# Six-layer local-attention transformer in one kernel: two output projections one step later, and three of them ahead of the turn

## The chip, the cores and the metric

The kernel runs on one core of one Trainium2 chip. The metric is the device time in microseconds (us). The core's engines are named as the profile names them: PE (TensorE; PEld is its weight load), DVE (VectorE), ACT (ScalarE), POOL (GpSimd) and SP (SyncE, which here only issues DMAs). Each engine runs its own instructions in the order written and waits on semaphores for the others.

## The reference

`x` is [2, 1024, 128]. Two blocks follow each other, `x = x + s * silu(g)`; in each, `s` is an attention over a layer norm of `x`, and `g` is in the first block a mixture of experts and in the second a transformer of six layers. The change touches only that transformer. One of its layers, with the tokens' right half of channels shifted by one token first:

```
qkv = shift(x) @ Wqkv                       # 128 -> 3 * 1024, 16 heads of 64
q, k = l2norm(q) * qs, l2norm(k) * ks, both rotated by a rotary table with scale
sim = 8 * q @ k^T, banded: query i sees keys i-32 .. i
x = softmax(sim) @ v @ Wo + x
a, gate = split(layernorm(shift(x)) @ W1 + b1)
x = (a * gelu(gate)) @ W2 + b2 + x
```

All of it is float32.

## The kernel before

The program is a sequence of stages. `stage_transformer` is the next to last; it takes the last 1976 us of a span of 3707 us.

**Passes and steps.** A pass `n` (0 to 23) does 8 of the 16 heads of one batch element in one layer. `j = n % 4` says which: half of the heads `h = j // 2`, batch element `b = j % 2`. A pass has 11 steps `s`, one for each tile of 96 queries. Token tiles of 128 (8 of them, `t`) are what is projected and turned. Passes with `j` 3 or 0, except pass 0, are *feeding*: they also carry the feed-forward of the batch element whose attention has just been finished, spread over their steps 0 to 5 (`feed_step`). There are 11 of these; the other 13 are called plain here. Passes 1 to 20 run in a hardware loop of five turns of four passes.

**What a step holds on PE**, in this order (`run` of the tensor block):

- `scores(n, s)` (L1943): 8 small products of keys and queries into banks SC0 and SC1. It waits until both copies of the youngest token tile that it reads are made (`qk_ready`). For step 1 that is the tile turned in step 0, for step 5 the one turned in step 4, for step 8 the one turned in step 7; in the other steps the tile was turned earlier.
- `weigh(n, j, s - 1)`: the softmax's sum (L1976, "den"), then weights times values (L1985, "num") for the tile before. It waits for the exponentials of that tile.
- `turn` (L1996) in steps 0 to 5, 7, 8 and, for the next pass, 10: PE transposes one token tile of normalized queries into bank X1, then of keys into bank X0; ACT copies each out (L2161 queries, L2164 keys).
- `project` (L1957, queries and keys into banks PQ and PK) and `values` (L1964, into X0, copied out by ACT L2138) in steps 1, 2, 3, 5, 6 and, for the next pass, 8, 9, 10.
- `project_out` (L2006): the output projection of 192 queries (the last one 64), four products that add up in X1. DVE adds the result to `x` (`add_out`, L2283), which frees X1 (`x_added`). It runs in steps 3, 5, 7, 9, and the last two parts in steps 0 and 1 of the next pass.
- in feeding passes the step's piece of the feed-forward: step 0 and 4 `up` (L2035, needs X0 and X1 both), step 1 and 5 `down` (L2045, X0), step 2 `mean_of` (L2014, X0), step 3 `variance` (L2020, X0).

**Banks.** X0 and X1 are shared by many users. `take(x)` makes PE wait until the last user of the bank has been read by its reader; `free[x]` holds which semaphore and count that is. A wait of PE stops all that is behind it.

**ACT in a step:** `invert` (L2143, L2145: logarithm and exponential of the softmax's sum, for the tile before), `roots` (L2150, L2152, L2155: the l2 norms of the tile projected in the step before), `copy_turned` (L2161, L2164), `squares` (L2129) and `copy_v` (L2138), `exps` (L2120: exponentials of this step's scores), and in feeding passes its part of the feed-forward (L2173, L2175 after the variance; the gelus L2181 with a table load).

**DVE in a step:** `mask` (L2266: scores plus band), `outputs` (L2274: num times the inverse sum), `rotate` (L2258, L2259, L2260, twice each: rotary products and sums of squares), `add_out` (L2283), and in feeding passes its part of the feed-forward (L2307, L2309 normalize; L2316 gate; L2323 feed).

**POOL** adds the rotary products and scales them into `nq` (L2421, L2428), which `turn` reads after waiting for `nq_ready`.

Of the kernel before, what the change touches and what calls it, by code (L numbers as in the profile page):

```python
# [11 lines left out]
P = 128  # L12
# [1741 lines left out]
WIN = 32  # L1754
# [10 lines left out]
OUTS = 6  # L1765
# [4 lines left out]
PROJ_NEXT_AT = {8: 0, 9: 1, 10: 2}  # L1770
TURN_AT = {0: 1, 1: 2, 3: 3, 4: 4, 5: 5, 7: 6, 8: 7}
TURN_NEXT_AT = {10: 0}
OUT_AT = {3: 0, 5: 1, 7: 2, 9: 3}


def out_width(e):
# [23 lines left out]
def stage_transformer(nc, d, ident, yT):  # L1800

    with Stage(nc, "tr") as st:
# [20 lines left out]
        qT = st.sb("qT", [P, NPAIR, S])  # L1823
        kT = st.sb("kT", [P, NPAIR, XW])
# [12 lines left out]
        ps = st.ps("ps", [P, 8, CH])  # L1837
# [6 lines left out]
        summed, nq_ready, turned, qk_ready = S_("summed"), S_("nq_ready"), S_("turned"), S_("qk_ready")  # L1844
# [13 lines left out]
        SC0, SC1, NUM, DEN, PQ, PK, X0, X1 = range(8)  # L1858
# [67 lines left out]
        def _(pe):  # L1926
            free = [None, None]
# [40 lines left out]
            def weigh(n, j, s):  # L1968

                a = NQT * n + s  # L1970
                width = tile_width(s)
                slot = (j + s) % 2
                pe.wait_ge(exp_done, a + 1)
                at_least(pe, o_ready, a)
                for e in range(2):
                    mm = pe.matmul(ps[e * DH:(e + 1) * DH, DEN, 0:NPAIR * QT], ones[:], pr[:, slot, e, :], start=True,  # L1976
                                   stop=True, tile_position=(0, e * DH), skip_group_check=True)
                mm.then_inc(den_done, 1)
                t = (QT * s + width - 1) // P
                for u in range(max(t - 1, 0), t + 1):  # L1980
                    pe.wait_ge(v_tiled[u % 2], 16 * tiled_count(n, u))
                for p in range(NPAIR):
                    for e in range(2):
                        head = 2 * p + e
                        mm = pe.matmul(ps[e * DH:(e + 1) * DH, NUM, p * QT:p * QT + width],  # L1985
                                       v[:, s, head * DH:(head + 1) * DH], pr[:, slot, e, p * QT:p * QT + width],
                                       start=True, stop=True, tile_position=(0, e * DH), skip_group_check=True)
                mm.then_inc(num_done, 1)

            def turn(n, t):  # L1990
                g = NTT * n + t
                for i, x in ((0, 1), (1, 0)):
                    take(x)
                    pe.wait_ge(nq_ready, 2 * g + 1 + i)
                    for p in range(NPAIR):
                        mm = pe.transpose(ps[:, X0 + x, p * P:(p + 1) * P], nq[:, t % 2, i, p * P:(p + 1) * P], ident[:])  # L1996
                    mm.then_inc(turned, 1)
                    free[x] = (qk_ready, 2 * g + 1 + i)

            def project_out(n, h, e):  # L2000
                width = out_width(e)
                slot = 2 * (e % 2) * QT
                take(1)
                pe.wait_ge(o_ready, NQT * n + min(2 * e + 2, NQT))
                for p in range(NPAIR):
                    mm = pe.matmul(ps[:, X1, 0:width], w[:, h, 3 * HC + p * P:3 * HC + (p + 1) * P],  # L2006
                                   o[:, p, slot:slot + width], start=(p == 0), stop=(p == NPAIR - 1))
                mm.then_inc(out_done, 1)
                free[1] = (x_added, OUTS * n + e + 1)
# [55 lines left out]
            def run(n, L, j, first=False, last=False):  # L2065
                h, b = j // 2, j % 2
                feeding = (j == 3 or j == 0) and not first
                if first:
                    for t in range(3):
                        project(0, 0, 0, t)  # L2070
                        values(0, 0, t)
                    turn(0, 0)
                free[0] = (qk_ready, 2) if first else (v_copied, NTT * n + 3)
                free[1] = (qk_ready, 2 * NTT * n + 1)
                for s in range(NQT):
                    scores(n, s)
                    if s:
                        weigh(n, j, s - 1)
                    elif not first:
                        weigh(n - 1, j - 1, NQT - 1)  # L2080
                    if s in TURN_AT:
                        turn(n, TURN_AT[s])
                    if s in TURN_NEXT_AT and not last:
                        turn(n + 1, TURN_NEXT_AT[s])
                    if s in PROJ_AT:
                        if feeding and s in (1, 5):
                            f = 2 * L if j == 3 else 2 * L - 1
                            pe.wait_ge(h_ready, 3 * (2 * f + s // 4) + 2)
                        project(n, L, j, PROJ_AT[s])
                        values(n, j, PROJ_AT[s])  # L2090
                    if s in PROJ_NEXT_AT and not last:
                        project(n + 1, L if j < 3 else L + 1, (j + 1) % 4, PROJ_NEXT_AT[s])
                        values(n + 1, (j + 1) % 4, PROJ_NEXT_AT[s])
                    if s in OUT_AT:
                        project_out(n, h, OUT_AT[s])
                    if s < 2 and not first:
                        project_out(n - 1, ((j - 1) % 4) // 2, OUTS - 2 + s)
                    if feeding:
                        feed_step(s, L if j == 3 else L - 1, 2 * L if j == 3 else 2 * L - 1,
                                  NTT * n + (3 if s == 0 else 6))  # L2100
                    if h == 1 and s == 8:
                        mean_of(2 * (2 * L + b), 0)
                    if h == 1 and s == 9:
                        variance(2 * (2 * L + b), 0)
# [4 lines left out]
            n = 4 * DEPTH  # L2109
# [7 lines left out]
        def _(act):  # L2117
# [37 lines left out]
                act.activation(rn[:, t % 2, :], rn[:, t % 2, :], ACT.Exp, scale=-0.5,  # L2155
                               bias=ln256[:, 0:1]).then_inc(rn_ready, 1)

            def copy_turned(n, t):
                g = NTT * n + t
                act.wait_ge(turned, 2 * g + 1)  # L2160
                act.copy(qT[:, :, t * P:(t + 1) * P], ps[:, X1, :].rearrange("p (a c) -> p a c", c=P)  # L2161
                         ).then_inc(qk_ready, 1)
                act.wait_ge(turned, 2 * g + 2)
                act.copy(kT[:, :, WIN + t * P:WIN + (t + 1) * P], ps[:, X0, :].rearrange("p (a c) -> p a c", c=P)  # L2164
                         ).then_inc(qk_ready, 1)

            def center_squares(k, c):
                act.wait_ge(centered, k + 1)
# [27 lines left out]
            def run(n, L, j, first=False, last=False):  # L2196
                h, b = j // 2, j % 2
                feeding = (j == 3 or j == 0) and not first
                if first:
                    for t in range(3):  # L2200
                        squares(0, t)
                        copy_v(0, t)
                        if t < 2:
                            roots(0, t)
                    copy_turned(0, 0)
                for s in range(NQT):
                    if s:
                        invert(n, s - 1)
                    elif not first:
                        invert(n - 1, NQT - 1)  # L2210
                    if s - 1 in PROJ_AT:
                        roots(n, PROJ_AT[s - 1])
                    if s - 1 in PROJ_NEXT_AT and not last:
                        roots(n + 1, PROJ_NEXT_AT[s - 1])
                    if s == 0:
                        roots(n, 2)
                    if s in TURN_AT:
                        copy_turned(n, TURN_AT[s])
                    if s in TURN_NEXT_AT and not last:
                        copy_turned(n + 1, TURN_NEXT_AT[s])  # L2220
                    if s in PROJ_AT:
                        squares(n, PROJ_AT[s])
                        copy_v(n, PROJ_AT[s])
                    if s in PROJ_NEXT_AT and not last:
                        squares(n + 1, PROJ_NEXT_AT[s])
                        copy_v(n + 1, PROJ_NEXT_AT[s])
                    exps(n, j, s)
                    if feeding:
                        feed_step(s, 2 * L if j == 3 else 2 * L - 1)
                    if h == 1 and s == 8:  # L2230
                        center_squares(2 * (2 * L + b), 0)
                    if h == 1 and s == 9:
                        deviations(2 * (2 * L + b), 0)
# [9 lines left out]
        def _(dve):  # L2243
# [112 lines left out]
            def run(n, L, j, first=False, last=False):  # L2356
# [5 lines left out]
                for s in range(NQT):  # L2362
# [7 lines left out]
                    if s in PROJ_NEXT_AT and not last:  # L2370
                        rotate(n + 1, PROJ_NEXT_AT[s])
                    if s in OUT_AT:
                        add_out(n, b, OUT_AT[s])
# [276 lines left out]
```

## Time and profile before

| | |
|---|---|
| median of 3 runs | 3710.39 us (3702.64 to 3718.77) |
| the profiled execution's own time | 3709.09 us |
| its span, first to last instruction | 3707.4 us |
| PE busy over the span | 2992.1 us (81%) |
| DVE, ACT, POOL busy | 2466.2 (67%), 2083.8 (56%), 1285.4 (35%) |
| mean granted TensorE clock | 0.906 |

Busy time is the time in which an engine's own instructions run; an engine that waits on a semaphore is not busy. Times of single instructions in the rows below are counted from the start of the span. PE's matmuls are pipelined: a group's listed duration reaches about 0.1 us into the next group, so the distance of two starts is what a group costs. In float32 each matmul shows as two records (x8 for four products).

### The profile page before, as it was taken

What the parts mean: (1) busy time and instruction counts of PE and PEld (TensorE: products, weight loads), DVE (VectorE), ACT (ScalarE), POOL (GpSimd) and SP (SyncE); (2) the same over time, 40 slices, a digit from 0 to 9 for tenths busy, and PEclk for the clock granted to TensorE, in tenths of its full rate; (3) what the DMA queues carried; (4) which work ended last, traced back from release to release, by engine and by line L of the source; (5) the groups of instructions that cost most, each with busy time, mean ns of one, the idle gap of its engine ahead of it and who ended that gap; (6) DMA issues with size and microseconds to landing.
All of it is one profiled execution on the core that took longest, in us unless ns stands there. A gap on an engine that the chain in (4) does not pass through costs nothing. (4 is left out here: it accounts for less than half of the span.)

```text
span 3707.4 us, 71470 instructions
## 1 busy us (share of the span) xinstructions
PE 2992.1 (81%) x22883; PEld 1620.1 (44%) x22883; DVE 2466.2 (67%) x4021; ACT 2083.8 (56%) x3805; POOL 1285.4 (35%) x1223
## 2 busy tenths in 40 slices
PE   2688887239738888845999999999999999999997
PEld 1332332113312223313665565566556556655653
DVE  6788888562347777765666666666666666666664
ACT  1477677112204666633666666666666666666664
POOL 0000000004323556624553354345435434544540
PEclk6588789569957999977999999999999999999998
DMA  5221121114231111232111111111111111111111
GB/s 197 84 85 55 62 73 60 56 45 108 67 38 30 35 34 34 37 68 99 38 54 31 49 54 31 42 45 51 34 49 49 35 42 45 49 31 53 38 35 42
DMA packets 195211, 200.31 MB, mean 54 GB/s; under 512 B 119077, under 2 KB 125877, under 8 KB 190090
## 3 DMA queue, kind: packets, MB, share of 16 engines
q1 hardware_dynamic: 193778, 195.46, 19.2%
q8 instruction: 209, 3.42, 0.4%
q14 instruction: 144, 1.18, 0.1%
q10 hardware_dynamic: 1080, 0.25, 0.0%
HBM read 99.84 MB, written 29.46 MB: 35 GB/s over the span
## 5 line engine op out<-in xcount | busy, mean ns | idle before, releaser
L2421 POOL TENSOR_TENSOR tr_t<-tr_t 128x512 f32<-128x512 f32 x384 | 489.7, 1275 | 683.5 <-DVE tr_t L2259 683.5
L2428 POOL TENSOR_TENSOR tr_nq<-tr_t,tr_rn 128x512 f32<-128x512 f32 x384 | 392.2, 1042 | 366.5 <-ACT tr_rn L2155 362.7
L1638 DVE TENSOR_REDUCE attn_mp<-attn_ps 128x1 f32<-128x512 f32 (+3 forms) x664 | 397.3, 656 | 146.4 <-PE attn_ps L1498 76.5
L2258 DVE TENSOR_TENSOR tr_t<-tr_ps,tr_tab 128x512 f32<-128x512 f32 x384 | 263.2, 685 | 241.1 <-ACT tr_sq L2129 241.1
L1957 PE MATMUL tr_ps<-tr_w,tr_xs 128*128 128x512 f32 x768 | 372.5, 607 | 25.0 <-DVE tr_xs L2292 21.8
L684 DVE TENSOR_REDUCE attn_mcol<-attn_ps 128x1 f32<-128x512 f32 x548 | 357.3, 681 | 50.2 <-PE attn_ps L529 40.4
L1600 ACT ACTIVATE attn_pr<-attn_ps 128x768 f32<-128x768 f32 (+2 forms) x352 | 294.9, 868 | 142.3 <-PE attn_ps L1521 140.0
L2143 ACT ACTIVATE tr_rd<-tr_ps 128x384 f32<-128x384 f32 x264 | 129.0, 489 | 376.1 <-PE tr_ps L1976 375.9
L1943 PEld LDWEIGHTS tr_ps<-tr_qT,tr_kT 64*128 64x128 f32 x4224 | 258.5, 188 | 176.6 <-issue 174.9
L1943 PE MATMUL tr_ps<-tr_qT,tr_kT 64*128 64x96 f32 (+1 forms) x4224 | 301.2, 282 | 31.4 <-ACT tr_kT L2164 20.1
L668 ACT ACTIVATE attn_pr<-attn_ps 128x512 f32<-128x512 f32 x512 | 272.6, 600 | 87.1 <-DVE attn_ps L706 68.9
L1449 POOL TENSOR_SCALAR_AFFINE_SELECT attn_pr<-attn_pr 128x256 f32<-128x256 f32 x256 | 220.0, 872 | 226.5 <-ACT attn_pr L1600 225.9
L2266 DVE TENSOR_TENSOR tr_pr<-tr_ps,tr_band 128x768 f32<-128x768 f32 x264 | 250.9, 950 | 59.5 <-PE tr_ps L1943 58.0
L2129 ACT ACTIVATE tr_sq<-tr_ps 128x512 f32<-128x512 f32 x384 | 227.2, 595 | 60.2 <-PE tr_ps L1957 58.8
L2259 DVE TENSOR_TENSOR tr_t<-tr_ps,tr_tab 128x512 f32<-128x512 f32 x384 | 261.0, 680 | 0.0
L2260 DVE TENSOR_REDUCE tr_ss<-tr_sq 128x8 f32<-128x512 f32 x384 | 259.1, 675 | 0.0
L1976 PE MATMUL tr_ps<-tr_pr,tr_ones 128*64 128x384 f32 x1056 | 230.8, 516 | 29.4 <-ACT tr_pr L2120 29.4
L1985 PEld LDWEIGHTS tr_ps<-tr_pr,tr_v 128*64 128x64 f32 x4224 | 204.9, 138 | 95.9 <-issue 89.2
L2006 PE MATMUL tr_ps<-tr_o,tr_w 128*128 128x192 f32 (+1 forms) x1152 | 205.3, 321 | 40.7 <-ACT tr_qT L2161 39.2
L529 PE MATMUL attn_ps<-attn_km,attn_qg 49*128 49x512 bf16 x548 | 158.7, 483 | 89.5 <-DMA attn_qg<-scratch_qp 50.3
L2006 PEld LDWEIGHTS tr_ps<-tr_o,tr_w 128*128 128x128 f32 x1152 | 184.1, 190 | 97.8 <-ACT tr_qT L2161 50.3
L2120 ACT ACTIVATE tr_pr<-tr_pr 128x768 f32<-128x768 f32 x264 | 224.0, 849 | 0.7 <-DVE tr_pr L2266 0.7
(257 smaller groups left out, 5177.0 us busy)
## 6 DMA issues: line engine op xcount, KB each, us to landing
tr_v<-tr_va SPq DMA_DIRECT2D x144, 192.0 KB, 2.6
attn_ka<-scratch_kp SPq DMA_DIRECT2D x72, 294.0 KB
tr_v<-tr_va SPq DMA_DIRECT2D x144, 128.0 KB, 2.2
moe_cb<-scratch_combineT SPq DMA_DIRECT2D x32, 512.0 KB
tr_w<-in_w_half SPq DMA_DIRECT2D x12, 1024.0 KB
tr_v<-tr_va SPq DMA_DIRECT2D x48, 256.0 KB, 2.4
scratch_kp<-proj_parts SPq DMA_DIRECT2D x36, 256.0 KB
attn_km<-scratch_kp SPq DMA_DIRECT2D x72, 98.0 KB
```

The lines of the kernel that those rows point to most:

```text
L668: act.activation(pr[:, a % 8, :], ps[:, unit % RING, :], ACT.Exp, scale=SCALE).then_inc(exp_done, 1)
L684: dve.tensor_reduce(mcol[:, (m // (2 * ST)) % 2, c, m % (2 * ST):m % (2 * ST) + 1], ps[:, MAXB + pos % MAXRING, :], AX.X, ALU.max).then_in ...
L1600: act.activation(pr[:, (UNITS * s + a) % PRU, :, 0:width], ps[:, 2 * (a % 2):2 * (a % 2) + 2, 0:width], ACT.Exp, scale=SCALE).then_inc(exp ...
L1638: dve.tensor_reduce(dst, src, AX.X, ALU.max).then_inc(maxed, 1)
L1943: mm = pe.matmul(ps[:, SC0 + e, p * QT:p * QT + width], kT[rows, p, s * QT:s * QT + P], qT[rows, p, s * QT:s * QT + width], start=True, st ...
L1957: pe.matmul(ps[:, PQ + i, :], xs[:, b, WIN + t * P:WIN + (t + 1) * P], w[:, h, i * HC:(i + 1) * HC], start=True, stop=True).then_inc(proje ...
L2006: mm = pe.matmul(ps[:, X1, 0:width], w[:, h, 3 * HC + p * P:3 * HC + (p + 1) * P], o[:, p, slot:slot + width], start=(p == 0), stop=(p == ...
L2258: dve.tensor_tensor(out[0], product, table[0], ALU.mult)
L2259: dve.tensor_tensor(out[1], product[:, :, ::-1, :], table[1], ALU.mult).then_inc(rope_done, 1)
L2260: dve.tensor_reduce(ss[:, slot, i * HH:(i + 1) * HH], sq[:, i, :].rearrange("p (h e) -> p h e", e=DH), AX.X, ALU.add).then_inc(ss_ready, 1)
L2421: pool.tensor_tensor(t12[:, slot, i, 0, :], t12[:, slot, i, 0, :], t12[:, slot, i, 1, :], ALU.add).then_inc(summed, 1)
L2428: pool.tensor_tensor(nq[:, slot, i, :].rearrange("p (h e) -> p h e", e=DH), t12[:, slot, i, 0, :].rearrange("p (h e) -> p h e", e=DH), rn[ ...
```

## The change

Four edits, all in the transformer:

1. `OUT_AT`: output projection 0 goes from step 3 to step 4, and 1 from step 5 to step 6. 2 and 3 stay in steps 7 and 9; 4 and 5 stay in steps 0 and 1 of the next pass.
2. In steps 0, 4 and 7 (`OUT_FIRST`) PE issues the output projection between `weigh` and `turn`, no longer behind `turn`. In step 0 that is part 4 of the pass before.
3. In these three steps `turn` transposes keys (into X0) first and then queries (into X1); both wait for the later of the two `nq_ready` counts. ACT's `copy_turned` follows the same order.
4. DVE's `add_out` has no edit of its own, but it goes by `OUT_AT`: it stands at the end of steps 4 and 6 instead of 3 and 5.

No instruction is added or taken away, and no DMA is moved.

```diff
-OUT_AT = {3: 0, 5: 1, 7: 2, 9: 3}
+OUT_AT = {4: 0, 6: 1, 7: 2, 9: 3}
+OUT_FIRST = (0, 4, 7)
...
-            def turn(n, t):
+            def turn(n, t, keys_first=False):
                 g = NTT * n + t
-                for i, x in ((0, 1), (1, 0)):
+                order = (1, 0) if keys_first else (0, 1)
+                for count, i in enumerate(order):
+                    x = 1 - i
                     take(x)
-                    pe.wait_ge(nq_ready, 2 * g + 1 + i)
+                    pe.wait_ge(nq_ready, 2 * g + 1 + max(order[:count + 1]))
                     for p in range(NPAIR):
                         mm = pe.transpose(ps[:, X0 + x, p * P:(p + 1) * P], nq[:, t % 2, i, p * P:(p + 1) * P], ident[:])
                     mm.then_inc(turned, 1)
-                    free[x] = (qk_ready, 2 * g + 1 + i)
+                    free[x] = (qk_ready, 2 * g + 1 + count)
...
+                    if s in OUT_AT and s in OUT_FIRST:
+                        project_out(n, h, OUT_AT[s])
+                    if s == 0 and not first:
+                        project_out(n - 1, ((j - 1) % 4) // 2, OUTS - 2)
                     if s in TURN_AT:
-                        turn(n, TURN_AT[s])
+                        turn(n, TURN_AT[s], s in OUT_FIRST)
...
-                    if s in OUT_AT:
+                    if s in OUT_AT and s not in OUT_FIRST:
                         project_out(n, h, OUT_AT[s])
-                    if s < 2 and not first:
-                        project_out(n - 1, ((j - 1) % 4) // 2, OUTS - 2 + s)
+                    if s == 1 and not first:
+                        project_out(n - 1, ((j - 1) % 4) // 2, OUTS - 1)
...
-            def copy_turned(n, t):
+            def copy_turned(n, t, keys_first=False):
                 g = NTT * n + t
-                act.wait_ge(turned, 2 * g + 1)
-                act.copy(qT[:, :, t * P:(t + 1) * P], ps[:, X1, :].rearrange("p (a c) -> p a c", c=P)
-                         ).then_inc(qk_ready, 1)
-                act.wait_ge(turned, 2 * g + 2)
-                act.copy(kT[:, :, WIN + t * P:WIN + (t + 1) * P], ps[:, X0, :].rearrange("p (a c) -> p a c", c=P)
-                         ).then_inc(qk_ready, 1)
+                for count, i in enumerate((1, 0) if keys_first else (0, 1)):
+                    dst = kT[:, :, WIN + t * P:WIN + (t + 1) * P] if i else qT[:, :, t * P:(t + 1) * P]
+                    act.wait_ge(turned, 2 * g + 1 + count)
+                    act.copy(dst, ps[:, X0 if i else X1, :].rearrange("p (a c) -> p a c", c=P)).then_inc(qk_ready, 1)
```

## Rows read from the trace of the kernel before

**Rows 1.** Windows view, the transformer: busy us (instructions) of PE, PEld, DVE, ACT, POOL; clock; DMA.

```profile
1711.00:3687.00 1976.00, 1822.26 (x13871) 1155.96 (x13872) 1292.59 (x2122) 1296.29 (x2520) 878.81 (x768) 0.99 0.14 42
```

**Rows 2.** Waits view: engine, line <- awaited: total us, times, longest.

```profile
PE tr_ps L2006 <- ACT tr_qT L2161: 39.2, 44, 1.0
PE tr_ps L1943 <- ACT tr_kT L2164: 20.1, 15, 1.4
```

**Rows 3.** Timeline (start, us, what, [idle <- releaser]), PE, plain pass, steps 2 to 5.

```profile
2467.84 1.02 PE L1964 MATMUL tr_ps<-tr_w,tr_xs 128*128 128x512 f32 x2
...
2470.36 0.87 PE L1976 MATMUL tr_ps<-tr_pr,tr_ones 128*64 128x384 f32 x4 [0.43 <-ACT tr_pr L2120]
...
2474.46 1.02 PE L1964 MATMUL tr_ps<-tr_w,tr_xs 128*128 128x512 f32 x2
2475.32 1.46 PE L2006 MATMUL tr_ps<-tr_o,tr_w 128*128 128x192 f32 x8
2476.72 1.14 PE L1943 MATMUL tr_ps<-tr_qT,tr_kT 64*128 64x96 f32 x16
2477.78 0.87 PE L1976 MATMUL tr_ps<-tr_pr,tr_ones 128*64 128x384 f32 x4
...
2479.24 1.09 PE L1996 MATMUL tr_ps<-ident,tr_nq 128*128 128x128 f32 x8
2481.72 1.14 PE L1943 MATMUL tr_ps<-tr_qT,tr_kT 64*128 64x96 f32 x16 [1.39 <-ACT tr_kT L2164]
...
2484.24 1.09 PE L1996 MATMUL tr_ps<-ident,tr_nq 128*128 128x128 f32 x8
```

**Rows 4.** Timeline, ACT, the same pass, steps 4 and 5.

```profile
2480.99 0.59 ACT L2164 COPY tr_kT<-tr_ps 128x512 f32<-128x512 f32 x1
...
2484.93 0.58 ACT L2161 COPY tr_qT<-tr_ps 128x512 f32<-128x512 f32 x1 [0.19 <-PE tr_ps L1996]
```

**Rows 5.** Timeline, DVE, the same pass, the end of step 3's rotation.

```profile
2477.77 0.67 DVE L2260 TENSOR_REDUCE tr_ss<-tr_sq 128x8 f32<-128x512 f32 x1
```

**Rows 6.** Timeline, PE, feeding pass 11, step 0.

```profile
2595.25 1.09 PE L1996 MATMUL tr_ps<-ident,tr_nq 128*128 128x128 f32 x8
...
2599.36 5.56 PE L2035 MATMUL tr_ps<-tr_xn,tr_w 128*128 128x512 f32 x12 [0.45 <-DVE xnT L2283]
```

**Rows 7.** Timeline, DVE, the same step.

```profile
2598.95 0.35 DVE L2283 TENSOR_TENSOR xnT<-xnT,tr_ps 128x192 f32<-128x192 f32 x1 [2.33 <-PE tr_ps L2006]
```

**Rows 8.** Timeline, PE, the same pass, steps 3 and 4.

```profile
2626.90 1.02 PE L1964 MATMUL tr_ps<-tr_w,tr_xs 128*128 128x512 f32 x2
...
2629.06 1.02 PE L2020 MATMUL tr_ps<-tr_sqf,tr_mean 128*128 128x512 f32 x2
...
2635.12 5.53 PE L2035 MATMUL tr_ps<-tr_xn,tr_w 128*128 128x512 f32 x12 [1.50 <-ACT tr_kT L2164]
```

**Rows 9.** Timeline, ACT, the same steps.

```profile
2628.04 0.59 ACT L2138 COPY tr_va<-tr_ps 128x512 f32<-128x512 f32 x1 [0.34 <-PE tr_ps L1964]
...
2630.12 0.69 ACT L2173 ACTIVATE tr_rstd<-tr_ps,tr_eps 128x512 f32<-128x512 f32 x1 [0.76 <-PE tr_ps L2020]
...
2634.28 0.59 ACT L2164 COPY tr_kT<-tr_ps 128x512 f32<-128x512 f32 x1
```

**Rows 10.** Timeline, DVE, the same steps.

```profile
2632.78 0.95 DVE L2266 TENSOR_TENSOR tr_pr<-tr_ps,tr_band 128x768 f32<-128x768 f32 x1
2633.65 0.55 DVE L2274 TENSOR_TENSOR tr_o<-tr_ps,tr_rd 128x384 f32<-128x384 f32 x1
```

**Rows 11.** Timeline, PE, the same pass, steps 5 to 8.

```profile
2645.75 1.02 PE L1964 MATMUL tr_ps<-tr_w,tr_xs 128*128 128x512 f32 x2
...
2647.91 2.74 PE L2045 MATMUL tr_ps<-tr_hid,tr_w 128*128 128x512 f32 x6
...
2657.36 0.87 PE L1976 MATMUL tr_ps<-tr_pr,tr_ones 128*64 128x384 f32 x4 [0.35 <-ACT tr_pr L2120]
...
2662.22 1.14 PE L1943 MATMUL tr_ps<-tr_qT,tr_kT 64*128 64x96 f32 x16
```

More of the change, by code:

```diff
@@ L2217, in run @@
                     if s in TURN_AT:
-                        copy_turned(n, TURN_AT[s])
+                        copy_turned(n, TURN_AT[s], s in OUT_FIRST)
                     if s in TURN_NEXT_AT and not last:
```

## Prediction

> **What bounds the kernel now.** The windows view comes first: in the 1976 us of the transformer PE is busy for 1822 us, DVE and ACT for 1293 and 1296, at a granted clock of 0.99, which is the upper level of 2.4 GHz [rows 1]. PE is the bound, and what the change can win is the rest: it adds and removes no matmul, so only PE's idle time can move. The waits view says whose idle time that is [rows 2]: 39.2 us in which the output projection waits for ACT's copy of the turned queries (its own bank X1 is full) and 20.1 us in which the scores wait for a copy. `up` waits for one in each of the 11 feeding steps 4, by 1.50 in the row shown, 16.5 us [rows 8]. These 76 us are 2% of the span and stand, by the timeline, in steps 0, 4/5 and 7. The timeline of a plain pass shows how [rows 3]: the turn of step 4 starts at 2479.24 and costs 0.93, then PE stands for 1.39 us until 2481.72. ACT is late there, since its `invert` and `roots` stand ahead of the copies; its second copy ends at 2480.99 + 0.59 = 2481.58 [rows 4].
>
> **The durations.** Out start to next start 2476.72 - 2475.32 = 1.40 behind a wait-free start, 1.35 taken before transposes; scores to den 1.06; den to what follows num 2479.24 - 2477.78 = 1.46; values to out 0.86 [rows 3]. Turn start to the end of its first bank, as ACT sees it, 2484.93 - 2484.24 = 0.69 [rows 3, 4]; a copy 0.58; copy end to scores 2481.72 - 2481.58 = 0.14 [rows 3, 4], and to `up` 2635.12 - (2634.28 + 0.59) = 0.25 [rows 8, 9]. `add_out` lasts 0.35 and PE goes on 0.06 after it: 2598.95 + 0.35 = 2599.30, `up` at 2599.36 [rows 6, 7]. An output projection that starts unhindered lasts 1.46 [rows 3], so `add_out` starts about 1.49 behind its start.
>
> **The new wait.** Where the output projection stands ahead of the turn, the keys' half goes at once into X0, but the queries' half needs X1, and X1 is free only when DVE has added the output. From the start of the output projection: keys turned 1.35 to 1.82; X1 free at 1.49 + 0.35 + 0.06 = 1.90; queries turned, as ACT sees it, 1.90 + 0.69 + 0.05 (a restart) = 2.64; ACT's second copy ends at 3.22; scores at 3.36, `up` at 3.47. So the order removes ACT's lateness from the path and puts a chain of PE, DVE, PE, ACT in its place; behind the waiting transposes stands all of PE. I take 3.33 for the scores. Bounds of the queries' wait: 0 (X1 free when the keys are through, 3.25) and, if DVE comes late, 0.4 more (outputs 0.55 minus what it overlaps).
>
> **Step 0, output projection 4.** It takes the place of the turn, T. Feeding pass: before, `up` is at T + 4.11 (2599.36 - 2595.25) [rows 6], for it waits for X1 behind the late output. After: T + 3.47 (3.45 to 3.5). Gain 0.65 x 11 = 7.2 us. Plain pass: the scores stand 0.10 ahead of where `add_out` starts, T + 3.60 [rows 6, 7]; after, T + 3.33. Gain 0.27 x 8 = 2.2 us. In the 4 plain passes that open a loop turn PE comes slow from the branch, at a lower clock, and the wait is nearly absent; the new chain costs there, I take 0.5 x 4 = +2 us. Pass 0 has no such projection: nothing. Sum -7.4 us.
>
> **Steps 3 and 4, plain (13 passes).** Without output 0 behind it, values of step 3 are followed by the scores at once, and den then meets the exponentials too early. The same is seen in step 2 to 3, which never had an output: den 2470.36 - 2467.84 = 2.52 behind values, with 0.43 of idle [rows 3]. So den comes at 2474.46 + 2.52 = 2476.98, only 0.80 ahead of the 2477.78 of now, not 1.40. Output 0 at + 1.46 = 2478.44, scores of step 5 at + 3.33 = 2481.77. Now: 2481.72 [rows 3]. DVE hides: its last reduce of the rotation starts at 2477.77 [rows 5], mask and outputs follow within 0.6 + 0.87 + 0.56 = 2479.8, ahead of the 2479.94 at which `add_out` can start. +0.05 x 13 = +0.6 us. The 1.39 us of idle are not won, they are split into 0.5 ahead of den and 0.9 ahead of the scores.
>
> **Steps 3 and 4, feeding (11).** Output 0 covers something here: `variance` needs X0, and X0 is freed by ACT's copy of the values, at 2628.04 + 0.59 = 2628.63, that is values + 1.73 [rows 8, 9]. Now `variance` is at + 2.16 (2629.06 - 2626.90), behind the output; after the change it waits until about + 1.85, and its successors come 0.1 later for the restart. PE: scores + 0.95 + 0.1, den + 1.06, output 0 + 1.46 = values + 5.42; by PE alone X1 would be free at + 7.3. DVE: the logarithm starts 1.06 behind `variance` [rows 8, 9], outputs 2633.65 - 2630.12 = 3.53 behind that, in an unbroken chain over normalization and mask [rows 9, 10], `add_out` 0.48 later: values + 1.85 + 0.1 + 1.06 + 3.53 + 0.48 = + 7.02, end 7.37. Queries turned from 7.43, seen 8.17, copied 8.75, `up` at + 8.95 to 9.0. Now: 2635.12 - 2626.90 = 8.22 [rows 8]. +0.73 x 11 = +8.0 us.
>
> VectorE's timing decides this place. Rows first: after a mask of 0.95 the outputs start 0.87 later [rows 10], so a DVE instruction begins before the last one's listed end. The Trainium skill ("VectorE: DVE Perf Modes", The DRAIN you can't avoid) says instead that each instruction is followed by a flush of its duration less 266 ns before the next may start. By that rule `add_out` would come 0.35 later behind outputs and the sum would be some 4 us higher, 3721; the rows above don't agree with it, and I keep the rows.
>
> **Steps 5 to 7, plain (13).** Step 5 loses output 1: scores of step 6 and den are again held by the exponentials, den at values + 2.52, now 0.86 + 1.40 + 1.06 = 3.32. Step 6 gains output 1: + 1.40, and loses the wait ahead of den in step 7 (listed 0.35, with the overlap 0.43 [rows 11]). Net - 0.80 + 1.40 - 0.43 = + 0.17; my count over the single starts gives + 0.08, I take 0.1. Step 7: scores of step 8 now come 2662.22 - 2657.36 = 4.86 behind den [rows 11], after 1.46 + 3.33 = 4.79, gain 0.07. Together 0 x 13 (0 to +1.3 us).
>
> **Steps 5 to 7, feeding (11).** Output 1 covered `down`'s wait for X0: now values + 2.16 (2647.91 - 2645.75 [rows 11]), after + 1.85, so 0.31 come back of 1.40, and 0.43 from den of step 7; a restart costs 0.03. + 1.40 - 0.31 - 0.43 + 0.03 - 0.07 (step 7) = +0.6, taken 0.54 x 11 = +5.9 us.
>
> **Sum.** -7.4 + 0.6 + 8.0 + 0 + 5.9 = +7.1 us. On the profiled execution's own 3709.09 us that is 3716.2; the median of the runs shown is 1.3 us above it, so I say 3717. What was said to be hidden: DVE's later mask in step 4 (ahead of `exps` by over 1 us), POOL's `nq` (done over 2 us before each turn), no DMA moves. PE's idle time stays some 76 us, but changes its places.
>
> **Rivals.**
> A, the waits simply go: X1 is back so early that nothing takes their place. 39.2 + 20.1 + 16.5 = 76 us off, 3634; if only half of it, 3672. For it: PE is the bound and its order is all that changes. Against: each of the three steps still ends in transposes, a copy of 0.58 and a reader, and steps 5 and 3 lose what covered X0.
> B, my chain is somewhat too long: the handoff over DVE and ACT takes 0.35 less at each of the 24 x 3 places. 71 x 0.35 = 25 us, 3717 - 25 = 3692, and with the restarts (0.05 to 0.1) 3685.
> C, slower: `add_out` is queued on DVE behind mask and outputs, and outputs behind ACT's inverse sum; if these are late in plain steps too, as I have them only in feeding step 4, the queries' turn comes 0.35 later at 71 places, +25 us: 3742. It decides from the point where outputs ends later than 1.5 us behind the output projection's start; by my count it ends 0.15 us ahead of it in plain step 4.
> D, the slow parts are only the feeding steps, but larger, 1.2 in place of 0.73 and 0.54: +12 us more, 3729.
>
> **Numbers.** About 0.5% (18.6 us) is what a measurement can tell from no change here. Forecast 3717 with its own range 3704 to 3730: 0.62. A 0.07, B 0.10, C 0.12, D 0.09. Faster by over 0.5%: A and most of B, 0.15. Slower by over 0.5%: C, half of D and the forecast's edge, 0.23. Within: 0.62. Range for 8 in 10: 3688 to 3742.
>
> **What would show it.** In the waits view the line of L2006 behind the queries' copy goes to almost nothing, and new lines stand for it: L1996 behind `add_out` (L2283, some 0.1 us a time, 0.2 or more in feeding step 4), L1943 and `up` behind the copy of the queries (L2161) near 1 us in steps 0, 4 and 7; L2020 and L2045 behind the copy of the values, 0.9 us, 11 times each; den (L1976) 0.4 to 0.5 in steps 4 and 6 of plain passes and gone in step 7. A plain pass keeps its length within 0.3 us, a feeding one grows by about 0.6. It is wrong if PE's idle time falls by more than 20 us, if L1996 waits over 0.3 us in plain steps, or if the turn starts to wait for `nq`.

## The result and the profile after

The changed kernel takes 3724.05 us (median of 20 runs, 3717.39 to 3731.07), the kernel before 3711.48 us (20 runs, 3702.64 to 3718.77). The ratio is 1.0036, 95% interval 1.0027 to 1.0044, so 10 to 16 us slower. The forecast was 3717, with 3688 to 3742 as its range, "within 0.5%".

The two profiled executions differ by more than the medians: 3725.0 - 3707.4 = 17.6 us of span, of which 9.2 lie between the transformer's first and last scores and 9.7 ahead of the first scores, where the code is the same; behind the last scores the changed one is 1.3 us shorter.

The first lines of the page and the transformer's row in the windows view (columns as in [rows 1]) of the changed kernel, profiled in a run of 3726.78 us:

```profile
span 3725.0 us, 71535 instructions
...
PE 3009.6 (81%) x22883; PEld 1621.0 (44%) x22883; DVE 2491.5 (67%) x4021; ACT 2100.3 (56%) x3805; POOL 1288.7 (35%) x1223
```
```profile
1720.00:3706.00 1986.00, 1831.66 (x13872) 1154.29 (x13872) 1318.22 (x2125) 1312.27 (x2520) 881.67 (x768) 0.99 0.14 42
```

As many PE, DVE, ACT and POOL instructions as before, the same granted clock of 0.99 in the transformer. The lines have moved: scores are L1944, den L1977, num L1986, the turn L1999, the output projection L2009, `up` L2038, `down` L2048, the variance L2023, `add_out` L2288, both turned copies L2170.

Who PE waited for (waits view: total us, times, longest), against [rows 2]:

```profile
PE tr_ps L1944 <- ACT tr_qT L2170: 38.9, 50, 1.3
PE tr_ps L1977 <- ACT tr_pr L2127: 31.7, 72, 2.0
...
PE tr_ps L2038 <- ACT tr_qT L2170: 16.9, 22, 0.8
PE tr_ps L2023 <- ACT tr_va L2145: 8.2, 11, 0.8
PE tr_ps L2048 <- ACT tr_va L2145: 8.2, 11, 0.8
...
PE tr_ps L1999 <- DVE xnT L2288: 3.1, 11, 0.3
```

The 39.2 us in which the output projection waited for the copied queries are gone, and so are 5 us of `up` behind the addition. The readers of the turn now wait 38.9 + 16.9 us for the last copy, before 20.1 + 16.8, and `variance` and `down` wait for their bank, 8.2 us each. All of PE's listed waits between the first and the last scores add up to 138.6 us before and 135.8 after: they changed their names and nearly kept their sum.

**A plain pass**, steps 3 to 5 (timeline, PE, pass 10; to be read beside [rows 3]):

```profile
2557.85 1.02 PE L1965 MATMUL tr_ps<-tr_w,tr_xs 128*128 128x512 f32 x2
2558.80 1.14 PE L1944 MATMUL tr_ps<-tr_qT,tr_kT 64*128 64x96 f32 x16
2560.37 0.87 PE L1977 MATMUL tr_ps<-tr_pr,tr_ones 128*64 128x384 f32 x4 [0.43 <-ACT tr_pr L2127]
...
2561.82 1.57 PE L2009 MATMUL tr_ps<-tr_o,tr_w 128*128 128x192 f32 x8
2563.23 1.27 PE L1999 MATMUL tr_ps<-ident,tr_nq 128*128 128x128 f32 x8
2565.26 1.14 PE L1944 MATMUL tr_ps<-tr_qT,tr_kT 64*128 64x96 f32 x16 [0.77 <-ACT tr_qT L2170]
```

Den comes 2.52 behind values (2560.37 - 2557.85), held by the exponentials, and the scores of step 5 are 7.41 behind values; before they were 2481.72 - 2474.46 = 7.26. The 1.39 us of idle are split in two, 0.43 and 0.77, and the rest shows as a longer listed output projection (1.57, not 1.46) and turn (1.27, not 1.09).

ACT and DVE behind that turn (timeline of each engine):

```profile
2563.86 0.59 ACT L2170 COPY tr_kT<-tr_ps 128x512 f32<-128x512 f32 x1 [0.65 <-PE tr_ps L1999]
2564.53 0.59 ACT L2170 COPY tr_qT<-tr_ps 128x512 f32<-128x512 f32 x1
```
```profile
2562.62 0.55 DVE L2279 TENSOR_TENSOR tr_o<-tr_ps,tr_rd 128x384 f32<-128x384 f32 x1
2563.43 0.35 DVE L2288 TENSOR_TENSOR xnT<-xnT,tr_ps 128x192 f32<-128x192 f32 x1 [0.27 <-PE tr_ps L2009]
```

Here the chain stands: output projection 2561.82, the addition at + 1.61 (DVE was idle for 0.27 and waited for PE, so PE gates it), its end at + 1.96, second copy at + 2.71, scores at + 3.44.

**A feeding pass**, steps 3 and 4 (timeline, PE; beside [rows 8]), then ACT and DVE (beside [rows 9, 10]):

```profile
2639.85 1.02 PE L1965 MATMUL tr_ps<-tr_w,tr_xs 128*128 128x512 f32 x2
2641.62 1.12 PE L2023 MATMUL tr_ps<-tr_sqf,tr_mean 128*128 128x512 f32 x2 [0.75 <-ACT tr_va L2145]
...
2645.20 1.57 PE L2009 MATMUL tr_ps<-tr_o,tr_w 128*128 128x192 f32 x8
2646.61 0.60 PE L1999 MATMUL tr_ps<-ident,tr_nq 128*128 128x128 f32 x4
2647.49 0.66 PE L1999 MATMUL tr_ps<-ident,tr_nq 128*128 128x128 f32 x4 [0.28 <-DVE xnT L2288]
2648.91 5.53 PE L2038 MATMUL tr_ps<-tr_xn,tr_w 128*128 128x512 f32 x12 [0.77 <-ACT tr_qT L2170]
```
```profile
2642.79 0.69 ACT L2178 ACTIVATE tr_rstd<-tr_ps,tr_eps 128x512 f32<-128x512 f32 x1 [0.47 <-PE tr_ps L2023]
...
2648.18 0.59 ACT L2170 COPY tr_qT<-tr_ps 128x512 f32<-128x512 f32 x1 [0.35 <-PE tr_ps L1999]
```
```profile
2644.17 1.09 DVE L2312 TENSOR_TENSOR tr_xn<-tr_xc,tr_rstd 128x512 f32<-128x512 f32 x1 [0.23 <-ACT tr_rstd L2180]
...
2645.76 0.95 DVE L2271 TENSOR_TENSOR tr_pr<-tr_ps,tr_band 128x768 f32<-128x768 f32 x1
2646.62 0.55 DVE L2279 TENSOR_TENSOR tr_o<-tr_ps,tr_rd 128x384 f32<-128x384 f32 x1
2647.09 0.35 DVE L2288 TENSOR_TENSOR xnT<-xnT,tr_ps 128x192 f32<-128x192 f32 x1
```

The turn is torn in two, and this time `add_out` waits for nothing: DVE is the late one, as forecast for this step alone. `up` starts at 2648.91, 9.06 behind values, before 8.22.

### The profile page after: what moved, and what is told of

Same layout as the page of the kernel before. It is cut to its first block and busy times, and to the rows that moved or that the text cites. A ratio compares the mean times of both kernels' runs of the same rounds, so it can differ in the third digit from the quotient of the medians.

```text
span 3725.0 us, 71535 instructions
## 1 busy us (share of the span) xinstructions
PE 3009.6 (81%) x22883; PEld 1621.0 (44%) x22883; DVE 2491.5 (67%) x4021; ACT 2100.3 (56%) x3805; POOL 1288.7 (35%) x1223
## 5 line engine op out<-in xcount | busy, mean ns | idle before, releaser
L1944 PEld LDWEIGHTS tr_ps<-tr_qT,tr_kT 64*128 64x128 f32 x4224 | 259.1, 188 | 196.7 <-issue 195.0
L1944 PE MATMUL tr_ps<-tr_qT,tr_kT 64*128 64x96 f32 (+1 forms) x4224 | 300.6, 282 | 51.0 <-ACT tr_qT L2170 38.9
L1977 PE MATMUL tr_ps<-tr_pr,tr_ones 128*64 128x384 f32 x1056 | 230.5, 515 | 31.7 <-ACT tr_pr L2127 31.7
L1986 PEld LDWEIGHTS tr_ps<-tr_pr,tr_v 128*64 128x64 f32 x4224 | 204.5, 138 | 95.7 <-issue 93.5
L1999 PE MATMUL tr_ps<-ident,tr_nq 128*128 128x128 f32 x1536 | 221.5, 280 | 4.9 <-DVE xnT L2288 3.1
L2279 DVE TENSOR_TENSOR tr_o<-tr_ps,tr_rd 128x384 f32<-128x384 f32 (+1 forms) x264 | 143.2, 542 | 110.3 <-ACT tr_rd L2152 108.7
```

Of the source, the lines that this page charges most:

```text
L1944: mm = pe.matmul(ps[:, SC0 + e, p * QT:p * QT + width], kT[rows, p, s * QT:s * QT + P], qT[rows, p, s * QT:s * QT + width], start=True, st ...
```

## The experiments

All steps' lengths below are differences of the starts of neighbouring scores groups in the PE timeline, against the same step and pass of the kernel before; medians over the 13 plain and the 11 feeding passes. The transformer's length is from the first to the last scores group of one profile; it also holds the steps that open a loop turn, one of which came out 3 us longer in one execution than in another (below). Ratios are to the kernel before, with their 95% intervals.

| run | ratio | plain pass | feeding pass | transformer, us |
|---|---|---|---|---|
| kernel before | 1 | 0 | 0 | 1917.5 |
| changed kernel, two profiles | 1.0036 (1.0027 to 1.0044) | +0.10 | +0.75 | +9.2, +11.7 |
| e1, step 0 alone | 0.9988 (0.9976 to 1.0) | -0.16 | -0.71 | -6.8 |
| e2, output 0 to step 4, ahead | 1.0018 (0.9997 to 1.0039) | +0.15 | +0.82 | +6.1 |
| e3, output 1 to step 6 | 1.0028 (1.0015 to 1.0041) | +0.07 | +0.59 | +4.3 |
| e4, step 7 alone | 1.0004 (0.9994 to 1.0014) | +0.03 | +0.03 | +0.4 |
| e5, queries first | 1.0128 (1.0104 to 1.0152) | +1.78 | +2.29 | +49.1 |
| e6, ahead, own bank | 0.9988 (0.9976 to 1.0) | -0.45 | -0.05 | -9.1 |
| e7, behind, own bank | 0.9816 (0.9799 to 0.9832) | -2.65 | -2.90 | -70.2 |
| e8, own bank in steps 0 and 7 | 0.9872 (0.9851 to 0.9893) | -1.84 | -2.63 | -52.1 |
| e9, output 0 to step 4, behind, own bank | 0.9955 (0.9939 to 0.997) | -0.80 | -0.51 | -18.0 |

**The changed kernel again.**

> The changed kernel again, as the yardstick beside its own parts. Theory (chain): where the output projection stands ahead of the turn, PE, DVE, PE and ACT follow each other before the next reader can start, and steps 3 and 5 lose their cover. It puts 9 us into the transformer: from the first scores to the last 1926.7 us, where the kernel before has 1917.5. Ratio to before 1.0025. Rival (elsewhere): the 12.6 us between the medians come mostly from outside the transformer; then the transformer's length differs from run to run by several us, or is the same.

Its ratio was 1.004 (1.0022 to 1.0057). Away from the loop's turns the step lengths of the two profiles agree within 0.04 us. Their transformers differ by 2.5 us, and one step after a branch makes that difference: step 0 of pass 13 took 5.85 us in one profile, with a granted clock of 1.00 throughout, and 8.97 in the other, where the clock was 0.50 for most of it. In both PE had done nothing for some 3 us at the branch.

**The four parts, one at a time.** Only two tables change; step 0's order follows `OUT_FIRST` too.

```diff
 e1  OUT_AT = {3: 0, 5: 1, 7: 2, 9: 3}   OUT_FIRST = (0,)
 e2  OUT_AT = {4: 0, 5: 1, 7: 2, 9: 3}   OUT_FIRST = (4,)
 e3  OUT_AT = {3: 0, 6: 1, 7: 2, 9: 3}   OUT_FIRST = ()
 e4  OUT_AT = {3: 0, 5: 1, 7: 2, 9: 3}   OUT_FIRST = (7,)
```

> Only step 0 is changed: output projection 4 ahead of the turn, keys first there; everything else as before. Theory (chain): this is the part that wins, 0.71 us in each of 11 feeding passes (up no longer waits for the addition behind a late output projection) and 0.16 in most plain ones: -9.6 us, ratio 0.9974, about 3702 us. Rival (the order as such is bad, whichever step has it): 0 to +3 us.

> Only output projection 0 is changed: step 4 in place of 3, ahead of the turn, keys first in step 4. Theory (chain): +0.15 us in 13 plain passes, +0.83 in 11 feeding ones, together +11 us, ratio 1.003. Rival (the loss is in the step-6 move): 0 us.

> Only output projection 1 is changed: step 6 in place of 5, no turn involved (step 7 keeps its old order). Theory (chain, lost cover): plain passes lose the wait ahead of the softmax sum in step 7 and gain one in step 6, +0.1 us x 13; in feeding passes down now waits for X0, +0.6 x 11; together +7.5 us, ratio 1.002. Rival (only the order ahead of the turn costs, moving is free): 0 us.

> Only step 7 is changed: output projection 2 ahead of the turn, keys first in step 7. Theory (chain): the scores of step 8 come 4.89 us behind the softmax sum of step 7, before 4.86: +0.03 x 24 = +0.7 us, no change that can be measured, although 19.5 us of waiting of the output projection vanish. Rival (waits simply go): 0.8 us x 24 = -19 us, ratio 0.995.

Each step changed where it should and nowhere else, and the parts add up: plain -0.16 + 0.15 + 0.07 + 0.03 = +0.09, feeding -0.71 + 0.82 + 0.59 + 0.03 = +0.73, against +0.10 and +0.75 in the changed kernel. Step 0 wins, 6.8 us by its profile and 0 to 9 by its ratio; the 9.6 expected had been summed over a profile whose loop turns came out shorter. Both moves lose. For e2 the steps' medians give 0.15 x 13 + 0.82 x 11 = +11 us, as expected; its profile has +6.1, since its loop turns came out short, and its ratio alone (-1 to +14 us) doesn't part it from no change. Step 7 shows the pattern best: the listed waiting ahead of its output projection, 0.81 x 24 = 19.5 us, vanishes, and the step grows by 0.03 us, for the scores behind it now wait instead. From the waits of e4:

```profile
PE tr_ps L1944 <- ACT tr_qT L2170: 18.4, 24, 0.8
```

The rival that waits simply go is refuted by e4, the rival that moving is free by e3.

**Queries first.** What the edit of the turn's order is worth.

```diff
-                        turn(n, TURN_AT[s], s in OUT_FIRST)
+                        turn(n, TURN_AT[s])
```

> The changed kernel with the queries turned first, as before, also in steps 0, 4 and 7 (the output projections stay ahead of the turn). Theory (chain): now all transposes wait for the addition that frees X1, and the second copy ends 0.48 us later (one copy behind another): scores and up come 0.45 to 0.5 us later at 71 places, +32 to +35 us against the changed kernel, ratio to before about 1.012. Rival (PE work decides, the order of keys and queries doesn't matter): the changed kernel's time.

With all transposes behind the addition, steps 0, 4 and 7 are each 0.56 us longer in plain passes than in the changed kernel, and 0.50, 0.49 and 0.56 in feeding ones, some 38 us, a little above the 32 to 35 expected. Turning keys first is a good edit: without it the change would have cost 49 us by the profiles, and not 9 to 12.

**A bank of its own.** In steps 0, 4 and 7 nothing is projected, and bank PQ is empty once DVE has rotated the tile of the step before.

```diff
+OUT_PQ = (0, 2, 4)
...
-                take(1)
+                x, bank = (2, PQ) if e in OUT_PQ else (1, X1)
+                if e in OUT_PQ:
+                    last = NTT * n + {0: 5, 2: 7, OUTS - 2: NTT - 1 if tail else NTT + 2}[e]
+                    pe.wait_ge(rope_done, 2 * last + 1)
+                take(x)
...
-                    mm = pe.matmul(ps[:, X1, 0:width], ...
+                    mm = pe.matmul(ps[:, bank, 0:width], ...
...
-                free[1] = (x_added, OUTS * n + e + 1)
+                free[x] = (x_added, OUTS * n + e + 1)
...
-                dve.tensor_tensor(yT[:, lo:lo + width], yT[:, lo:lo + width], ps[:, X1, 0:width],
+                dve.tensor_tensor(yT[:, lo:lo + width], yT[:, lo:lo + width], ps[:, PQ if e in OUT_PQ else X1, 0:width],
```

`last` is the youngest token tile in PQ. `project` and `up` wait by `take(2)` before they write PQ. Where both turned copies are awaited with queries first (e5, e7, e8, e9), `up` waits for the later count alone, which implies the other. In feeding step 4 of e8 that is the only edit, and the step is 0.17 to 0.26 us shorter, some 2 us in all, which the own bank didn't win. e6 is this with the changed kernel's order; e7 has the turn first and queries first, and `OUT_AT = {4: 0, 5: 1, 7: 2, 9: 3}`; e8 is `OUT_PQ = (2, 4)` with all places of before; e9 is e7 with `OUT_PQ = (0,)`.

> The changed kernel, but output projections 4, 0 and 2 (steps 0, 4, 7) write to bank PQ, which is empty there, so the queries' turn waits for no addition. Theory (chain): only the DVE link falls out: 0.15 to 0.2 us at 60 places, 0.5 to 0.6 in the 11 feeding steps 4, together -15 us against the changed kernel, which is some 5 us below before: ratio 0.9985. Rival (the wait for the addition is the whole loss): as much as all idle time behind the turns, -50 us.

> The old order (turn first, queries first), output projections 4, 0 and 2 behind the turn in steps 0, 4 and 7, but in bank PQ, so none of them waits for ACT's copies; output 0 in step 4, output 1 stays in step 5. Theory (chain): the output projection of 1.35 us lies beside ACT's copies. Scores follow in step 7 3.94 us behind the softmax sum, before 4.86 (-0.92 x 24 = -22 us), in step 0 -0.9 x 12 = -11, up in step 0 -1.3 x 11 = -14, steps 3 and 4 -0.8 x 13 and -0.2 x 11 = -13: -60 us, ratio 0.984, about 3652 us. Rival (PE is held by something else next, DVE or the exponentials): half of that or less.

> The old order and the old places of all output projections; only 4 (step 0) and 2 (step 7) write to bank PQ in place of X1. Theory (the shared bank made the output projection wait for ACT): step 0 -0.93 us in plain and -1.53 in feeding passes, step 7 -0.92, as in the kernel with all three in PQ: 54 us, 3657 us, ratio 0.9855. Rival (the gain needs output 0 in step 4 as well): less than 40 us.

> Only output projection 0 is changed: step 4 in place of 3, behind the turn, in bank PQ. The counterpart to the same move ahead of the turn, which cost 6 to 8 us. Theory (the move itself pays when nothing waits behind it): -0.80 us in 13 plain passes and -0.45 in 11 feeding ones, -15 us, ratio 0.996; with the run of steps 0 and 7 alone it adds up to the 70 us of all three. Rival (lost cover in step 3 eats the gain): 0.

e6 takes DVE out of the chain. Against the changed kernel each of the 60 places is 0.18 us shorter and feeding step 4 is 0.44, together 16 us where 15 were expected (18 to 21 by the profiles), not the 50 of the rival: with the output projection ahead, PE still turns last and ACT still copies last, and the readers still wait 0.82 us each for that copy, 59 us in all. e7 is the fastest kernel of the study, 3642.65 us (5 runs, 3637.81 to 3643.76), 69 us below the kernel before, where 60 were expected: `up` in step 0 gained 1.53, not 1.3, and feeding steps 3 and 4 gained 0.45, not 0.2. Its step 7 (timeline, PE, then ACT):

```profile
2537.15 0.87 PE L1980 MATMUL tr_ps<-tr_pr,tr_ones 128*64 128x384 f32 x4 [0.35 <-ACT tr_pr L2137]
...
2538.61 1.09 PE L2002 MATMUL tr_ps<-ident,tr_nq 128*128 128x128 f32 x8
2539.54 1.47 PE L2016 MATMUL tr_ps<-tr_o,tr_w 128*128 128x192 f32 x8
2541.09 1.14 PE L1945 MATMUL tr_ps<-tr_qT,tr_kT 64*128 64x96 f32 x16
```
```profile
2539.90 0.57 ACT L2180 COPY tr_qT<-tr_ps 128x512 f32<-128x512 f32 x1
2540.36 0.59 ACT L2180 COPY tr_kT<-tr_ps 128x512 f32<-128x512 f32 x1
```

Scores follow den by 3.94 us (2541.09 - 2537.15) as expected, before 4.86. The output projection now runs while ACT copies. The waits for the copies in e7:

```profile
PE tr_ps L1945 <- ACT tr_kT L2180: 5.1, 13, 1.3
PE tr_ps L2047 <- ACT tr_kT L2180: 3.1, 11, 0.3
```

8.2 us, where the changed kernel has 55.8. e8 and e9 add up to e7 in the profiles, 52.1 + 18.0 = 70.1.

The order and the bank can now be told apart. In step 7, against the kernel before (behind the turn, shared bank): ahead in the shared bank +0.03 (e4), ahead in its own bank -0.14 (e6, -0.57 less the -0.43 that moving output 1 brings in e3), behind in its own bank -0.92 (e8). The own bank wins much only behind the turn. For output 0 in step 4, steps 3 and 4 over all passes come to +11 us ahead in X1 (e2), +4 ahead in PQ (e6) and -15 behind in PQ (e9), of which some 2 are `up`'s single wait.

## Why the prediction was right

Measured per pass, against the prediction's own terms:

| term | predicted | measured |
|---|---|---|
| step 0, feeding | -0.65 | -0.71 |
| step 0, plain | -0.27 | -0.16 |
| steps 3 and 4, plain | +0.05 | +0.15 |
| steps 3 and 4, feeding | +0.73 | +0.83 |
| steps 5 to 7, plain | 0 | +0.11 |
| steps 5 to 7, feeding | +0.54 | +0.63 |
| the four plain steps 0 that open a loop turn, together | +2 us | -0.5 us, +2.6 us |
| transformer | +7.1 us | +9.2 us, +11.7 us |

The mechanism held: the waits were exchanged, not won; e4 shows it with one step alone. Five of the six terms came out about 0.1 us too favourable, for three reasons.

In the plain passes it is one mis-sized piece. I took 1.49 us from the start of an unhindered output projection to its addition, from the listed 1.46 in [rows 3]. Behind num it lists 1.57, and the addition comes at + 1.61. The chain to the scores is 3.44, not 3.33. The kernel before lists 1.57 too, at the 44 output projections that had waited; the prediction doesn't use it.

In feeding steps 5 to 7 the same 0.10 stands in step 7, and it is made up ahead of it: `down` starts at values + 1.77, not 1.85, and e3 measures +0.59 where the prediction's terms without step 7 give 0.69. Its terms as written add up to 0.62, which is what came; only the value taken, 0.54, was too low. The third reason is feeding step 4, below.

Two smaller errors went the other way: `up` starts 0.14 behind the copy, not 0.25 (2648.91 behind 2648.18 + 0.59), and `variance` starts at values + 1.77, not 1.85.

That the total came so close is in part luck. Without the four plain steps that open a loop turn, the terms predicted add up to +5.1 us and those measured to +10.4. The +2 us taken for these four measured -0.5 in one profile of the changed kernel and +2.6 in the other, and the clock there differs between them, so no run shows that term.

**Feeding step 4.** DVE gates the turn as forecast, but the chain that leads there was wrong in one link. From the logarithm to outputs it took 3.83 us (2646.62 - 2642.79), not 3.53, since the normalization took 1.09 us, not 0.79. DVE's normalization and POOL's addition in the kernel before, then POOL's addition in the changed one, whose normalization (2644.17) is shown above:

```profile
2631.50 0.79 DVE L2307 TENSOR_TENSOR tr_xn<-tr_xc,tr_rstd 128x512 f32<-128x512 f32 x1 [0.26 <-ACT tr_rstd L2175]
2630.47 1.27 POOL L2421 TENSOR_TENSOR tr_t<-tr_t 128x512 f32<-128x512 f32 x1 [0.51 <-DVE tr_t L2259]
```
```profile
2643.43 1.28 POOL L2426 TENSOR_TENSOR tr_t<-tr_t 128x512 f32<-128x512 f32 x1 [0.52 <-DVE tr_t L2264]
```

The normalization ends 0.55 us behind the end of POOL's addition both times (2632.29 behind 2631.74, 2645.26 behind 2644.71), and POOL's addition ends 4.84 and 4.86 behind values: it did not move. So the earlier `variance` brought nothing: outputs start at values + 6.75 before and + 6.77 after, where the prediction had + 6.54.

**The flush of VectorE.** Outputs began 0.86 behind a mask of 0.95, and the addition 0.47 behind outputs of 0.55. The rows were the right side to keep. By an estimate from the figure of the Trainium skill ("VectorE: DVE Perf Modes", The DRAIN you can't avoid), the addition would have come at outputs + 0.83. The prediction left out how that paragraph ends: a next op that is not held starts earlier. With that the page leaves room for what the rows show.

**The signs the text had named.** The wait of L2006 for the copied queries went; those of `variance` and `down` came, 0.75 each time, forecast 0.9; den's wait left step 7 and came in plain steps 4 and 6, 0.43 each; the readers of the turn wait 0.77 each, forecast near 1. The turn's wait for `add_out` is listed only in feeding step 4; the small ones elsewhere are inside the turn's longer duration, 1.27 - 1.09 = 0.18 us a time, forecast some 0.1.

**What stays open.** The transformer accounts for 9.2 and 11.7 us in two profiles, the medians differ by 12.6, the interval is 10 to 16. e3 shows the same: +4.3 in its profile, +6 to +15 by its ratio. The stages ahead have the same code and end at different times: the first scores group starts between 1726.1 and 1739.0 us in the eleven profiles of changed kernels, at 1729.2 in the one of before. No experiment tells whether some 3 us of the slowdown lie there, or whether that is scatter. Why an output projection lists 1.57 us in one place and 1.46 in another is open too.

## What to carry to other kernels

When a wait stands ahead of an instruction, ask what holds the next reader: here it was the last copy behind the turn, so reordering PE moved the wait, and a free bank removed it only where the output projection stood behind the turn. Long independent work belongs between a producer and the reader of its copy, not ahead of the producer: in its own bank, output 0 in step 4 cost 4 us ahead of the turn and won some 13 behind it. And a piece that seems badly placed may cover a bank's turnaround: where it leaves, the next user of that bank shows the wait. An earlier start wins nothing where the next engine is bound by a third one: there the end of POOL's addition decided.

## What the runs showed of the hardware

The same output projection (four products of 192 columns) lists 1.46 to 1.47 us where it follows 512-wide products or transposes and waits for nothing (values in [rows 3], the turn in e7, with the addition 1.50 behind its start), and 1.57 where it follows num or has waited, with the addition 1.61 behind. Width does not decide it, for transposes are narrow too; behind values and behind num alike, PE's next group starts 1.39 to 1.41 us behind its start.

A DVE instruction that lists a start while POOL works can be held to POOL's end. In all twelve profiles the normalization of 512 elements, both of whose inputs lie in SBUF, takes 0.69 us where POOL covers at most 0.09 us of it (146 cases). In the other 142 cases, where it lists its start over 0.15 us ahead of the end of POOL's addition, it ends 0.546 to 0.557 us behind that end, whatever its own start, and so lists up to 1.14 us. DVE's rotary products, which read a bank and a table, list 0.68 us with or without POOL beside them. No run takes POOL away, but a constant distance to POOL's end over all these starts leaves little else.
